# A Swin block on one core: the products behind the late weights in two parts, earlier in the prologue and later in tile 1

## The reference

```python
xn = ln2d(x, norm1_g, norm1_b)                    # over the 64 channels of each pixel
windows = partition(roll(xn, (-4, -4)), 8)        # 64 windows of 64 pixels
q, k, v = split(windows @ in_w.T + in_b)          # 8 heads of 8
attn = softmax(q @ k.T / sqrt(8)) @ v             # in each window and head
y = x + unroll((attn @ out_w.T + out_b) @ proj_w.T + proj_b)
z = ln2d(y, norm2_g, norm2_b)
out = y + (gelu(z @ fc1_w.T + fc1_b) @ fc2_w.T + fc2_b)
```

## Time and profile before

| | |
|---|---|
| median of 3 runs | 97.44 us (97.42 to 100.54) |
| profiled execution | 97.66 us, span 95.8 us |
| TensorE busy | 86.4 us, 90% |
| VectorE busy | 63.8 us, 67% |
| ScalarE busy | 48.1 us, 50% |
| GpSimd busy | 43.5 us, 45% |
| granted TensorE clock, mean | 0.997 |
| `masked` copies on the SP queue | 58 of 32 KB |

### The profile page before, as it was taken

One profiled execution on the slowest core, in us unless ns is written; L12 is line 12 of the kernel. 1 busy time (PEld: TensorE's weight loads), 2 busy tenths in 40 slices (PEclk: granted clock), 3 DMA queues, 4 the chain that ended last, 5 costly groups with the idle time before them and its releaser, 6 DMA issues.

```text
span 95.8 us, 4276 instructions
## 1 busy us (share of the span) xinstructions
PE 86.4 (90%) x1810; PEld 55.0 (57%) x1810; DVE 63.8 (67%) x183; ACT 48.1 (50%) x78; POOL 43.5 (45%) x56
## 2 busy tenths in 40 slices
PE   5999999999999699999999889989899967799960
PEld 5987756776755557747666567566665224233330
DVE  5966879818899978957959889798342943403070
ACT  0594815735556447556655443335449654073700
POOL 7988734485056436750740834708343063500000
PEclk9999999999999999999999999999999999999998
DMA  2899110111110111111110101000000000020323
GB/s 36 236 383 403 64 42 14 57 48 42 41 46 29 61 42 56 36 47 42 34 61 28 61 28 41 0 7 0 7 0 7 0 0 7 0 109 0 113 107 112
DMA packets 3747, 5.87 MB, mean 61 GB/s; under 512 B 1136, under 2 KB 1904, under 8 KB 3600
## 3 DMA queue, kind: packets, MB, share of 16 engines
q1 hardware_dynamic: 2864, 3.22, 9.9%
q10 hardware_dynamic: 864, 2.38, 6.6%
HBM read 2.64 MB, written 1.05 MB: 39 GB/s over the span
## 4 chain that ended last, share of the span: by engine, by line
PE 32%; issue 24%; POOL 19%; DVE 15%; DMA 3%; SPq 2%; POOLq 1%; ACT 1%; DVEq 0%
POOL max_x L937 7%; POOL rstd L946 7%; PE ps_t L257 6%; DVE row_max L594 6%; POOL rstd_x L953 5%; DMA masked<-qk 3%; PE ps_t L359 3%; PE ps_u L449 3%; PE ps_m L277 3%; DVE sums L608 2%; PE ps_s L302 2%; PE ps_t L433 2%; PE ps_o L449 2%; PE ps_u L376 2%; SPq L238 2%
## 5 line engine op out<-in xcount | busy, mean ns | idle before, releaser
L825 ACT ACTIVATE probs<-ps_t 128x1024 f32<-128x1024 f32 x16 | 16.4, 1024 | 17.4 <-PE ps_t L359 17.4
L594 DVE TENSOR_REDUCE row_max<-ps_s 128x16 f32<-128x1024 f32 x15 | 18.2, 1216 | 5.2 <-PE ps_s L302 5.2
L302 PE MATMUL ps_t<-masked,qk 32*64 32x256 f32 x272 | 18.7, 387 | 0.4 <-ACT probs L825 0.3
L946 POOL TENSOR_TENSOR rstd<-y_var,minus_half 128x4 f32<-128x4 f32 x8 | 8.3, 1034 | 22.0 <-DVE y_var L642 21.8
L302 PE MATMUL ps_s<-masked,qk 32*64 32x256 f32 x240 | 16.5, 386 | 1.7 <-ACT probs L825 0.7
L359 PE MATMUL ps_t<-max_x,minus_sel 128*128 128x512 f32 x32 | 11.7, 446 | 0.8 <-POOL max_x L937 0.8
L302 PEld LDWEIGHTS ps_s<-masked,qk 32*64 32x64 f32 x240 | 8.3, 131 | 4.3 <-issue 2.8
L376 PE MATMUL ps_u<-probs,vz 128*32 128x64 f32 x512 | 10.5, 222 | 0.0
L376 PEld LDWEIGHTS ps_u<-probs,vz 128*32 128x32 f32 x512 | 7.9, 109 | 3.8 <-issue 2.8
L302 PEld LDWEIGHTS ps_t<-masked,qk 32*64 32x64 f32 x272 | 8.7, 131 | 1.5 <-issue 0.4
L257 PE MATMUL ps_t<-zeros 128*128 128x128 f32 x40 | 8.2, 366 | 1.0 <-DVE zeros L737 1.0
(11 more groups left out here) (102 smaller groups left out, 147.8 us busy)
## 6 DMA issues: line engine op xcount, KB each, us to landing
masked<-qk SPq DMA_DIRECT2D x58, 32.0 KB, 1.9
x_ch<-x_ch_d ACTq DMA_DIRECT2D x1, 1024.0 KB, 8.5
out_d<-result SPq DMA_DIRECT2D x3, 256.0 KB, 2.5
x_tok<-x_tok_d ACTq DMA_DIRECT2D x1, 512.0 KB, 6.5
late<-late_d ACTq DMA_DIRECT2D x1, 352.0 KB, 5.1
x_tok<-x_tok_d SPq DMA_DIRECT2D x2, 128.0 KB, 3.2
x_tok<-x_tok_d ACTq DMA_DIRECT2D x1, 256.0 KB, 4.5
out_d<-result SPq DMA_DIRECT2D x2, 128.0 KB, 2.3
```

Source lines behind the costliest of these rows:

```text
L302: return nc.tensor.matmul(ps[L * u:L * u + L, g, n * TOK:(n + 1) * TOK], qk[r:r + RG, b, w, t], masked[r:r + RG, b, :, w, t], start=(n == ...
L594: nc.vector.tensor_reduce(row_max[:, 16 * w:16 * w + 16], score_bank(k, w)[:].rearrange("q g (h j) -> q (g h) j", j=L), axis=AX.X, op=ALU. ...
L825: nc.scalar.activation(probs[:, w, :], ps_t[:].rearrange("q g c -> q (g c)"), ACT.Exp).then_inc(probs_done, 1)
L946: nc.gpsimd.tensor_tensor(rstd2[:].rearrange("q n w -> q (n w)"), y_var[:].rearrange("q n w -> q (n w)"), minus_half[:], op=ALU.pow).then_ ...
```

## The change

`late_products` becomes two functions. `late_products_out` (the waits, the output matrix, the output bias; L457 and L459) moves ahead to just behind `project_qk(0)`, in place of two of the four filling products there. `late_products_bias` (L462, L464, and the semaphore) goes into `first_slot` ahead of `project_qkv(2)`, in place of two filling products. The other changes: the two filling products ahead of `scores(0, 0)` go, the two ahead of `first_slot` become one, and the two behind the late products go; `scores(1, 1)` stands ahead of `weigh_values(0, 0)`; `fc1_mean` and `bias_of_v` move from the end of `first_slot` into TensorE's slot 1, behind `shift_scores(1, 0)`; `late_bias` moves from the end of VectorE's slot 0 into its slot 1, behind `find_max(2, 0)`. All products of weights and biases are still made, once.

```diff
-            def late_products():
+            def late_products_out():
                 pe.wait_ge(late_loaded, 16)
                 pe.wait_ge(b_qk_made, 1)
                 nc.tensor.matmul(ps_o[:, 0, 0:C], out_w_x, proj_w_t, start=True, stop=True)
                 for w in range(2):
                     nc.tensor.matmul(ps_o[C * w:C * w + C, 0, C:C + 1], proj_w_t, vec[0:C, OUTB:OUTB + 1],
                                      start=True, stop=True)
+
+            def late_products_bias():
                 for m in range(M2):
...
                 scores_t(0, 0)
                 shift_scores(0, 0)
                 x_transpose(2)
-                warm_up(2, ps_u)
+                late_products_bias()
                 project_qkv(2)
-                late_products()
-                warm_up(2, ps_u)
                 scores_both(1, 0, 0, 1)
                 shift_scores(0, 1)
                 x_transpose(3)
+                scores(1, 1)
                 weigh_values(0, 0)
-                scores(1, 1)
                 project_qkv(3)
-                fc1_mean()
-                bias_of_v()
...
                 shift_scores(t, 0)
                 if t == 1:
+                    fc1_mean()
+                    bias_of_v()
                     weigh_values(0, 1)
...
             project_qk(0)
-            warm_up(4)
+            late_products_out()
+            warm_up(2)
             project_v(0)
-            warm_up(2)
             scores(0, 0)
             x_transpose(1)
             scores(0, 1)
             project_qkv(1)
-            warm_up(2, ps_u)
+            warm_up(1, ps_u)
             first_slot()
...
                 if t == 0:
                     late_weights()
-                elif tile_ok(t + AHEAD + 2):
+                if t == 1:
+                    late_bias()
+                if t >= 1 and tile_ok(t + AHEAD + 2):
                     ln1_stats(t + AHEAD + 2)
...
                     ln1_stats(AHEAD + 2)
-                    late_bias()
                     dve.wait_ge(vz_zeroed, 2)
```

## The result

The changed kernel takes 96.03 us in the median of four runs (95.81 to 100.3), the kernel before 97.46: a ratio of 0.9847, with a 95% interval of 0.981 to 0.9884. The profiled execution went from 97.66 to 95.85 us, its span from 95.8 to 94.0: 1.8 us, where 1.84 was forecast (95.6, range 95.1 to 97.3).

A forecast was written before the change was run, and what follows sets the result against it. The order in which results are handed on was taken as the bound: TensorE to 24 us, VectorE from 24 to 33. Tile 1's scores gain 1.86, 1.84 reaches the end: 97.44 − 1.84 = 95.6 us, range 95.1 to 97.3.

The forecast's parts named there:

- Nothing to gain before 15.2: Prologue: tile 0's last query copy still ends at 15.21, so earlier edits gain nothing; up to 0.9 us TensorE idle.
- 17.06 to 20.49: TensorE around tile 2's projection: fewer fillers and late products, so tile 1's scores start at 18.63, 1.86 us earlier.
- 19.8 to 23.7: First slot: find_max(1,1) at 22.26, project_qkv(3) at 22.70, tile 2's scores at 23.65 instead of 25.69.
- rival B: Slot 1: a slow key copy of tile 2 delays bias_of_v and late_bias by 0.6 us; 96.0 to 96.9, chance 0.20.
- 24 to 33: Slots 0 and 1: late_bias takes 0.42 plus 0.06 us wait; find_max(2,1) at 30.09, 1.84 us earlier.
- To the end: From slot 2 on nothing in the program changes, so the 1.84 us gain should arrive at the end.
- Rival D: TensorE's clock falls to 1.2 GHz at 15 us after idling, costing 1.9 or 3.8 us (97.5 or 99.4); chance 0.06.
- Rival C: SP queue: tile 3's copies issue only 0.8 to 0.9 us earlier and set the pace; 96.6 us, chance 0.10.
- Rival E: First stages save 2.0 to 2.3 us and late_bias is hidden on VectorE; 95.1 to 95.4 us, chance 0.12.

The follow-up runs named there:

- the second profile: The changed kernel, unaltered, run again beside the kernel before ("changed, again" in the table); profiled run 96.60 us, ratio 0.9843.
- the two profiles above: Changed kernel with fc1_mean and bias_of_v back in TensorE's first slot, and that with half of late_bias in VectorE's slot 2; profiled executions 97.29 and 99.54 us.
- fillers_gone: The kernel before with the nine filling products taken away that the change takes away, nothing moved; ratio 0.9925.
- fillers_kept: The changed kernel with all nine filling products put back; 97.7 us, ratio 0.9992 to the kernel before.
- wide_fillers: The changed kernel with its early fillers as fewer, wide products of the same total columns, 40 TensorE instructions fewer; ratio 0.9849 to the kernel before.
- wide_best: Changed kernel with wide fillers, 384 columns before first slot, fc1_mean and bias_of_v in TensorE's first slot, half of late_bias in VectorE's slot 2; 95.12 us, ratio 0.9739.

## Why the prediction was right, point by point

- **Nothing to gain before 15.2.** Right: the query copy ended at 15.04. That it ends so late was taken as given; it is one packet of the instruction queue that makes it so, and the number of instructions ahead decides when that packet comes. The idle time it left was 0.65 us here and 0.97 in the second profile, for the 0.9 given.
- **17.06 to 20.49.** 18.63 forecast, 18.56 measured, with the copy 0.17 earlier than before. From one start of tile 0's scores to tile 1's the step is 3.48 us, 5.23 before: 1.75 gained, 0.1 less than the 1.86 summed. The bias products cost 0.2 ahead of the projection and not 0.11: before, the projection had waited for its input, and that input came 0.17 earlier too. The forecast start was met because that 0.1 and the 0.17 by which the copy landed earlier, on which the forecast had not counted, cancelled: that much is luck.
- **19.8 to 23.7.** `find_max(1,1)` 22.26 forecast, 22.16 measured; `project_qkv(3)` 22.70 and 22.60; the scores of tile 2 at 23.65 and 23.89, with a masked copy as the releaser, inside the 23.6 to 24.0 that was kept for the range. The 0.39 us of idle time before it is over the 0.3 that was to be the sign of rival B; in this profile it cost little, since `find_max(2,0)` has no idle time before it and only `late_bias` waits a little longer (next point).
- **24 to 33.** `find_max(2,0)` 25.60 and 25.55; `late_bias` at about 26.8 and 26.90, its wait some 0.2 us (26.69 to 26.90) and not 0.06; `find_max(2,1)` 30.09 and 30.20; slot 2's scores 31.4 and 31.49. This was the decisive step: of 2.37 us that VectorE had gained at `find_max(2,0)`, 0.64 were gone at the next maximum, 0.48 forecast.
- **To the end.** Forecast as 1.84 passed on in full: 1.72 at slot 2, 1.78 at the last result.
- **The median** is 0.4 above the forecast (96.03 for 95.6), its profiled execution 0.05 (95.85 for 95.8). Half of the 0.4 is the run of 100.3, which the median counts: that of the other three is 95.85. The profiled execution had the early query copy; with the copy of the second profile the span is 94.8 and the gain 1.0. That spread is rival B, which I had as an alternative: in one run the key copy of tile 2 and the query copy of tile 0 cost hardly anything, in another 0.8 us more together, and `late_bias` waited for `bias_of_v` as B says. B's price for the key copy was near (0.6 for a copy of 3.3 us; 0.47 measured, for one of 3.1), the chance was wrongly put as one or the other, and the query copy, taken to land "as before", is not in it.
- **Rival D, the clock,** was real and undervalued at 0.06: about one run in four of the kernels with that idle time. It cost about 1 to 4.5 us by the runs' times, and in the two profiles above spans of 95.5 for 94.0 and of 97.7 where the runs of that kernel at full clock had 93.4 to 93.9. The changed kernel's own run of 100.3 us is slower than the 97.5 of the kernel before, so the gain of 1.5% holds for runs in which the clock stays up. Against D I set a stretch of the kernel before in which TensorE was busy 1.22 of 2.00 us at full clock; one stretch that went well says nothing about another one, in the prologue. The Trainium skill ("TensorE: Matmul & The Clock Gate", section "A second HAM failure mode: psum-queue depth-cycling") tells of a kernel whose clock went up and down because the array idled briefly and often. The 13 runs of 48 agree with it in that idle times of about 1 us can be enough; in the two profiles here it was one such idle time, and the clock fell once and rose again.
- **Rival C** did not happen: no masked copy on the chain after 23.85. **Rival E** neither: VectorE's front at `find_max(2,0)` was 2.37, as E had it, but `late_bias` was not hidden.

## What to carry to other kernels

Follow the path stage by stage and ask in each which list the moved work joins: here 0.84 us of TensorE work and 0.42 of VectorE's were moved from one place on the path to another, and nearly all of the gain came from the products and fillers that left it. A filling product that stands off the path is not free to drop: where they were dropped and about 1 us of idle time was left, the clock fell in 13 runs of 48, and where that time was filled or short in none of 27. Their number counts too, since it moves the instruction packets: wide ones cleared the query copy's way here, and the next packet then held a key copy, so look at the whole row of packets before counting on it. Where a small transfer lands 3 us after issue and its fellows after 1.8, look for a packet of the instruction queue beside it.

## What the runs showed of the hardware

**Instruction packets and data share DMA engines.** One 16 KB packet for some 256 TensorE instructions, 0.9 to 1.7 us long. In the eleven profiles with narrow fillers 15 of the 16 data packets of the fourth query copy, issued at 11.91 to 11.98, start before 13.5 us, and the sixteenth within 0.02 us of the end of the first instruction packet. The copy landed 1.02 to 1.17 us after that end, wherever it was. In the three profiles with wide fillers all 16 start before 13.5:

| kernel | first instruction packet | copy landed |
|---|---|---|
| changed | 12.98 to 13.98 | 15.04 |
| before | 12.97 to 14.04 | 15.21 |
| changed, again | 12.99 to 14.34 | 15.36 |
| fillers_gone | 13.56 to 14.49 | 15.57 |
| fillers_kept | 13.72 to 14.65 | 15.73 |
| wide_fillers | 13.67 to 14.81 | 13.75 |
| wide_best | 13.67 to 14.60 | 13.76 |

In fillers_kept the instruction packet started as late as in wide_fillers, 0.3 us after the copy's other packets, and still held the last one; what kept that one waiting before 13.72 is not to be seen in these traces, and stays open. Nor do they name the engine of a packet: that the two share one is inferred from the times. That TensorE's instruction count sets the time is shown for the first packet: 40 instructions fewer ahead of it, 0.7 us later in the same program, and in all fourteen profiles it starts when 192 to 216 weight loads and products have begun. That is one way in which an edit off the path changes a kernel's time.

**The clock fell after idle times of 0.8 to 1.1 us** in some runs of a program and not in others of the same one (to 0.50 in the two profiles shown, at a cost of 1.5 and 4 us), although TensorE had been busy 5.68 of the 5.80 us from 8.3 to 14.1. Four profiles show a fall, with 0.80, 1.00, 1.04 and 1.11 us of idle time before tile 0's scores; three with 0.86, 0.96 and 0.97 show none. So the length alone does not decide it; what does is open.
